# A decoder block on one core: the weights' preparation ahead of the attention loop, rearranged

## The reference

```python
def _act_quant(x):
    s = 127.0 / jnp.clip(jnp.max(jnp.abs(x), axis=-1, keepdims=True), 1e-05)
    return jnp.clip(jnp.round(x * s), -128.0, 127.0) / s
def _weight_quant(w):
    s = 1.0 / jnp.clip(jnp.mean(jnp.abs(w)), 1e-05)
    return jnp.clip(jnp.round(w * s), -1.0, 1.0) / s
qkv = _bitlinear(x, w_qkv).reshape(B, N, 3, H, D)       # both quantized, then x @ w.T
attn = softmax(causal(q @ k.T * D ** -0.5))             # 16 heads of 32
out = _bitlinear(attn @ v, w_proj)
x = x + out; x = x + xattn(layernorm(x), k, bias, ctx); x = x + ffn(layernorm(x))
```

## Time and profile before

| | us |
|---|---|
| three runs | 1494.40, 1491.86, 1492.63 |
| median | 1492.63 |
| profiled execution, span from first to last instruction | 1492.0 |
| PE busy | 1397.0 (94%) |
| DVE busy | 1238.3 (83%) |
| POOL busy | 1181.3 (79%) |
| ACT busy | 867.5 (58%) |
| first `row_max`, t=0 | 61.7 |
| first `low_part`, t=11 | 88.75 |
| end of the last `low_part`, about | 472 |

### The profile page before, as it was taken

One profiled execution on the slowest core, in us unless ns is written; L12 is line 12 of the kernel. 1 busy time (PEld: TensorE's weight loads), 2 busy tenths in 40 slices (PEclk: granted clock), 3 DMA queues, 4 the chain that ended last, 5 costly groups with the idle time before them and its releaser, 6 DMA issues.

```text
span 1492.0 us, 23946 instructions
## 1 busy us (share of the span) xinstructions
PE 1397.0 (94%) x8405; PEld 775.2 (52%) x8405; DVE 1238.3 (83%) x1965; ACT 867.5 (58%) x1433; POOL 1181.3 (79%) x903
## 2 busy tenths in 40 slices
PE   3589999999987898899999999999999999999998
PEld 2478787878764443334444444444444444444443
DVE  5789999999984799889998899899889889898511
ACT  3589999999977223444545455454455446544341
POOL 2379999999986687888888878878887888788432
PEclk9799999999998899999999999999999999999999
DMA  4556464646431633212422321332322232240001
GB/s 144 138 134 157 134 171 133 178 127 165 113 99 48 184 92 84 71 50 71 99 50 50 93 78 43 78 82 60 78 64 71 63 79 57 64 99 14 17 20 29
DMA packets 171587, 133.57 MB, mean 90 GB/s; under 512 B 120500, under 2 KB 124748, under 8 KB 171468
## 3 DMA queue, kind: packets, MB, share of 16 engines
q1 hardware_dynamic: 171276, 131.91, 33.5%
q10 hardware_dynamic: 192, 0.14, 0.1%
HBM read 50.67 MB, written 19.92 MB: 47 GB/s over the span
## 4 chain that ended last, share of the span: by engine, by line
PE 64%; DVE 12%; POOL 8%; ACT 7%; issue 7%; DMA 1%; POOLq 0%; SPq 0%; DVEq 0%; ACTq 0%
PE gu L788 20%; PE gu L802 10%; PE shared_bank L733 9%; PE y L755 3%; PE y L749 3%; PE y L752 3%; PE y L757 3%; PE y L758 3%; POOL pL L1696 3%; DVE blockmax L917 2%; DVE o_sb L957 1%; DVE z L1148 1%; ACT pH L1353 1%; DVE qkt L897 1%; ACT pT L1347 1%
## 5 line engine op out<-in xcount | busy, mean ns | idle before, releaser
L1576 ACT ACTIVATE shared<-shared_bank 128x512 f32<-128x512 f32 x162 | 96.2, 594 | 339.9 <-PE shared_bank L733 339.9
L1145 DVE TENSOR_TENSOR y<-shared,y 128x512 f32<-128x512 f32 x324 | 224.1, 692 | 46.4 <-ACT shared L1576 24.6
L1696 POOL TENSOR_TENSOR pL<-pT,pH 128x768 f16<-128x768 f32 x128 | 216.5, 1693 | 11.1 <-ACT pH L1353 4.9
L788 PE MATMUL gu<-fT,wu 128*128 128x512 f16 x768 | 183.0, 381 | 0.0
L1152 DVE TENSOR_REDUCE oT<-z 128x64 f32<-128x512 f32 x256 | 175.6, 686 | 8.8
L788 PE MATMUL gu<-fT,wg 128*128 128x512 f16 x768 | 181.4, 379 | 1.0 <-DMA fT<-fnl 1.0
L1148 DVE TENSOR_TENSOR z<-y,cT 128x512 f32<-128x512 f32 x236 | 162.4, 688 | 11.6 <-PE y L747 5.3
L1834 POOL TENSOR_TENSOR fuL<-fu,fuH 128x512 f16<-128x512 f32 x96 | 112.3, 1170 | 71.6 <-ACT fuH L1591 71.4
L802 PE MATMUL gu<-wd,fuH 128*128 128x512 f16 x384 | 145.8, 380 | 0.0
L802 PE MATMUL gu<-wd,fuL 128*128 128x512 f16 x384 | 145.6, 379 | 0.0
L1770 POOL TENSOR_TENSOR kv<-vT,cT 128x1024 f32<-128x1024 f32 x70 | 137.9, 1971 | 5.2 <-ACT vT L1531 5.2
(11 more groups left out here) (216 smaller groups left out, 3564.6 us busy)
## 6 DMA issues: line engine op xcount, KB each, us to landing
pack<-qkhl SPq DMA_DIRECT2D x256, 128.0 KB, 2.4
x_sb<-in_x SPq DMA_DIRECT2D x16, 512.0 KB, 4.0
c_sb<-in_ctx SPq DMA_DIRECT2D x32, 256.0 KB, 3.8
hankel<-in_L_xattn_k SPq DMA_DIRECT2D x32, 256.0 KB, 4.1
out_y<-yo SPq DMA_DIRECT2D x32, 256.0 KB, 2.8
x_grp<-x_scratch SPq DMA_DIRECT2D x30, 256.0 KB, 3.4
x_scratch<-x_sb SPq DMA_DIRECT2D x14, 512.0 KB, 2.8
...
```

The lines of the kernel that those rows point to most:

```text
L788: made = T.matmul(bank[:], (wg, wu)[which][:, cb, ib * P:(ib + 1) * P], fT[:, cb, part, :], start=cb == 0 and part == 0, stop=cb == CB - 1 ...
L1145: chain.step(V.tensor_tensor(bank[:], shared[2 * part + half][:], bank[:], op))
L1696: G.tensor_tensor(pL[n % 2][:], pT[n % NP][:], pH[n % NP][:], ALU.subtract).then_inc(low_done, 1)
```

## The change

Sums: chunks 0 and half of 2 are summed by DVE, chunk 1 and the other half of 2 by ACT (`ACT.Abs` with an accumulated output). Chunk 3 is summed by DVE at the end of the prologue. Ternary weights: q's chunk is made by ACT alone (`round_weights(0)`, then a new `sign_weights(0)`), k's by DVE alone (three passes in `ternary(1)`), at the same time; v's by DVE alone (`ternary(2)`), w_proj's by ACT alone, in the loop at t=2. Turning: k first (all four copies by DVE), then q (all four by ACT), in the prologue; v's at t=-3 and -1, w_proj's at t=3 and 4, copied a step later in alternation. The products of batch 0 alternate between q and k. Of the 16 DMAs that pack batch 0, SP issues 8 and ACT 8 (`pack_rest`). v of batch 0 is computed at t=4 and 6, not 0 and 2; piece 0 of the gate weights passes four steps later. POOL fills `pick` and other constants after `power_in(0)`. SP holds back the loads of x(1) and w_proj until chunk 1 is in.

```diff
+        FIRST_V_AT, FIRST_V_SPLIT_AT = (17, 19), (18, 20)
+        V_WEIGHTS_AT, PROJ_WEIGHTS_AT, LOAD_PIECES_AT = (-3, -1), (3, 4), 5
...
+        W_ORDER = (1, 0, 2, 3)
+        def wT_by_act(i, ob):
+            return i == 0 or (i >= 2 and ob % 2 == 0)
+        def turning(t):
+            for i, at in ((2, V_WEIGHTS_AT), (3, PROJ_WEIGHTS_AT)):
+                if t in at:
+                    yield i, range(2 * at.index(t), 2 * at.index(t) + 2)
+        def qk_groups(s):
+            return s % 2, 2 * (s // 2)
...
 tensor_program
-            weight_total([0, 1, 2], 0)
-            turn_weights(0)
-            spread_c(0)
+            bank = misc1.take("tab", w, (tab_done, 1))
+            w.wait_ge(tables_in, 48)
+            T.transpose(bank[:, 0:2 * IB], rows_s[:], ident[0:2 * IB, 0:2 * IB]).then_inc(tab_pe, 1)
+            weight_total(0, 4, 0)
             for j in range(2):
                 turn_xq(0, j)
             turn_weights(1)
+            turn_weights(0)
+            spread_c(0)
             for g2 in range(4):
                 multiply_qk(0, g2)
-            weight_total([3], 1)
-            turn_weights(2)
-            turn_weights(3)
-            spread_c(1)
             for j in range(2):
                 turn_xq(1, j)
+            spread_c(1)
...
+                for i, blocks in turning(t):
+                    turn_weights(i, blocks)
+                if t == V_WEIGHTS_AT[-1]:
+                    weight_total(4, 1, 1)
                 for b, k in project_steps(t):
                     if k < 4:
                         multiply_qk(b, k)
...
 vector_program
             def ternary(i):
-                w.wait_ge(wround_done, i + 1)
+                chain.step(V.tensor_scalar(wraw[i][:], wraw[i][:], ws[:, 1:2], ROUND, ALU.mult, ALU.add))
+                chain.wait()
                 chain.step(V.tensor_scalar(wraw[i][:], wraw[i][:], ROUND - 1.0, ROUND + 1.0, ALU.max, ALU.min))
...
+            magnitude(0, WB, 0)
             max_in(0)
+            magnitude(2, WB // 2, 2)
             scale_in(0)
+            weight_scale(4, 3, 0, 0)
+            ternary(1)
...
+            copy_weights(1)
             stats_in(1)
+            scale_qk(0, 0)
+            scale_qk(0, 1)
+            max_in(1)
+            scale_qk(0, 2)
+            scale_qk(0, 3)
+            scale_in(1)
             ternary(2)
+            magnitude(3, WB, 4)
...
+                for i, blocks in turning(t - 1):
+                    copy_weights(i, blocks)
+                if t == V_WEIGHTS_AT[-1] + 1:
+                    weight_scale(1, 1, 2, 1)
...
 scalar_program
+            def magnitude(i, first, col):
+                w.wait_ge(wraw_in[i], 16)
+                S.activation(tern[i - 1][:, first:WB, :], wraw[i][:, first:WB, :], ACT.Abs, accum_out=wsums[:, col:col + 1]).then_inc(wsum_act, 1)
+            def sign_weights(i):
+                w.wait_ge(act_step, 1 if i == 0 else 2)
...
+                S.activation(tern[i % 2][:], wraw[i][:], ACT.Sign, bias=minus_round[:]).then_inc(tern_act, 1)
+            def pack_rest():
+                w.wait_ge(qk_high, 4)
+                w.wait_ge(qk_low, 4)
+                for r in (2, 3):
+                    for j in range(4):
+                        S.dma_start(packs[0][j * D:(j + 1) * D, :, r, :, :], ...).then_inc(packed[0], 16)
...
             moments(0)
             normalise(0)
+            magnitude(1, 0, 1)
             step_in(0)
+            magnitude(2, WB // 2, 3)
             for i in range(NT):
                 round_in(0, i)
+            round_weights(0)
             diagonal(0)
+            sign_weights(0)
+            for j in range(2):
+                copy_xqT(0, j)
             copy_weights(0)
             copy_c(0)
             moments(1)
             normalise(1)
+            high_qk(0, 0)
+            high_qk(0, 1)
             step_in(1)
+            high_qk(0, 2)
+            high_qk(0, 3)
             for i in range(NT):
                 round_in(1, i)
+            pack_rest()
             diagonal(1)
...
+                if t == PROJ_WEIGHTS_AT[0] - 1:
+                    round_weights(3)
+                    sign_weights(3)
...
 sync_program
-                for r in range(R):
+                for r in range(R) if b > 0 else (0, 1):
...
+            w.wait_ge(wraw_in[1], 16)
             load_x(1)
...
+            pack_qk(0)
...
-                if t == 0:
+                if t == LOAD_PIECES_AT:
                     load_piece(0)
                     load_piece(1)
```

More of the change, by code:

```diff
@@ L497, in tensor_program, with turn_weights @@
             w = Waits(tensor)
-            def turn_weights(i):
-                for ob in range(WB):
-                    freed = (wT_act, 2 * i + ob // 2 + 1) if ob % 2 == 0 else (wT_dve, 2 * i + ob // 2 + 1)
+            def turn_weights(i, blocks=range(WB)):
+                for ob in blocks:
+                    by_act = wT_by_act(i, ob)
                     w.wait_ge(const_done, C_BASE)
-                    bank = misc1.take(("wT", i, ob), w, freed)[:].bitcast(BF16)
-                    w.wait_ge(tern_done, i + 1)
+                    bank = misc1.take(("wT", i, ob), w, (wT_act if by_act else wT_dve, wT_copies(i, ob, by_act)))[:].bitcast(BF16)
+                    if i in (1, 2):
+                        w.wait_ge(tern_dve, i)
+                    else:
+                        w.wait_ge(tern_act, 1 if i == 0 else 2)
                     for cb in range(CB):
@@ L507, in turn_weights, with weight_total @@
                     made.then_inc(wtr_pe, 1)
-            def weight_total(pieces, use):
-                n = len(pieces)
-                bank = misc1.take(("wtot", use), w, (wscale_done, use + 1))
+            def weight_total(first, n, use):
+                bank = misc1.take(("wtot", use), w, (wscale_done, 2 * use + 1))
                 w.wait_ge(const_done, C_BASE)
-                w.wait_ge(wsum_done, pieces[-1] + 1)
-                T.matmul(bank[:, 0:n], ones[:], wsums[:, pieces[0]:pieces[0] + n], start=True, stop=True).then_inc(wtot_pe, 1)
+                w.wait_ge(wsum_dve, 2 + use)
+                w.wait_ge(wsum_act, 2)
+                T.matmul(bank[:, 0:n], ones[:], wsums[:, first:first + n], start=True, stop=True).then_inc(wtot_pe, 1)
             def spread_c(b):
@@ L1229, in scale_down @@
             def scale_down():
-                w.wait_ge(down_in, 16)
+                w.wait_ge(tables_in, 64)
                 chain.wait()
@@ L1319, in round_weights @@
-                S.activation(wraw[i][:], wraw[i][:], ACT.Copy, bias=ROUND, scale=ws[:, 2 * use + 1:2 * use + 2]).then_inc(wround_done, 1)
-            def copy_weights(i):
-                dst, o_first = (wqkvT, i * C) if i < 3 else (wprojT, 0)
-                for ob in range(0, WB, 2):
-                    w.wait_ge(wtr_pe, WB * i + ob + 1)
-                    src = misc1.of["wT", i, ob][:].bitcast(BF16)[:, 0:CB * P].rearrange("p (c o) -> p c o", c=CB)
-                    S.activation(dst[:, :, o_first + ob * P:o_first + (ob + 1) * P], src, ACT.Copy).then_inc(wT_act, 1)
+                w.wait_ge(wscale_done, 2 * use + 1)
@@ new lines, in copy_weights @@
+            def copy_weights(i, blocks=range(WB)):
+                dst, o_first = (wqkvT, i * C) if i < 3 else (wprojT, 0)
+                for ob in blocks:
+                    if wT_by_act(i, ob):
+                        w.wait_ge(wtr_pe, w_turned(i, ob))
+                        src = misc1.of["wT", i, ob][:].bitcast(BF16)[:, 0:CB * P].rearrange("p (c o) -> p c o", c=CB)
+                        S.activation(dst[:, :, o_first + ob * P:o_first + (ob + 1) * P], src, ACT.Copy).then_inc(wT_act, 1)
@@ L1713, in gpsimd_program @@
             power_in(0)
+            set_pick()
+            set_once()
+            power_in(1)
             for g2 in range(4):
                 low_qk(0, g2)
[L1716 to L1723 removed]
             for t in STEPS:
```

182 lines of the change are left out of this document (87 added, 95 removed).

## The result

The changed kernel takes 1504.24 us (median of 4 runs, 1504.13 to 1504.32), the kernel before, beside it, 1493.26 (4 runs, 1491.86 to 1494.4). The ratio is 1.0073, interval [1.0059, 1.0087]: 0.73% slower. The forecast was 1496.0 with a range up to 1500.5, so the sign of the likeliest case was right and the size wrong by 8 us.

The account below looks back on a forecast made before the run. It took POOL as the pace from t=11, DVE just before, batch 2's input ahead of that. -8.1 + 3.9 + 1.8 + 4.1 + 1.8 = +3.5 us on 1492.0, plus 0.6 to the median, gave 1496.0, range 1486.5 to 1500.5.

Parts of the forecast that it names:

- the six terms of the table: Forecast shifts from `max_in(2)` through `take_max(0)`, `take_max(4)`, `low_part(0)`, `low_part(8)` to the last `low_part`: -8.1, +3.9, +1.8, +4.1, +1.8, 0 us.
- Scale, q's and k's weights, packing start: Prologue: scale ready at 16.7 us, `multiply_qk(0)` at 26.7, packing from 37.35, instead of 18.34, 32.41 and 40.98.
- I take the middle, 48.2: Batch 2's statistics start at 48.2 us, between 46.5 (load alone) and 50.0; so `max_in(2)` at 53.0, -8.1.
- the bound 50.0 for shared DMA engines: Batch 2's statistics start at 50.0 us if 16 packing DMAs hold the DMA engines 9.3 us, whoever issues; sum 1.8 worse.
- Steps up to `take_max(0)`, 8.7: `max_in(2)` to `take_max(0)`: 8.7 us instead of 4.75, +3.9 (+1.0 to +4.5), as turned weights take banks among products.
- `take_max(0)` to `take_max(4)`, 12.6: 12.6 us instead of 10.75, +1.8 (+0.4 to +2.5): PE waits for ACT's two w_proj passes before turning its blocks.
- `take_max(4)` to `low_part(0)`, +4.1: +4.1 us (0 to +4.7): DVE's v splits and piece 0's mask and clamp now come at t=5 to 7.
- POOL, "0 to +3.6, I take +1.8": After `low_part(0)`: piece 0's add and take, 1.82 us each, move to steps 15 and 16, where POOL is full; +1.8.
- Later, 0: From `low_part(8)` to the last `low_part`: no further change, 0 us.
- (3): Rival, much slower: ports hold POOL's last low part (+2.4), shared DMA engines delay batch 2 (+1.8); 1500.3 us, chance 0.10.
- (2): Rival, faster: ACT's pair and bank waits hidden, steps lose only DVE's added work; -6.1 to -4.4, 1487.4 us, chance 0.28.

Follow-up runs that it names:

- e14_before_x_early: The kernel before with only x(2) loaded ahead of the first batch's packing; 1493.55 us.
- e2_x2_early: The changed kernel with x(2) loaded right behind w_proj, ahead of the packing; 1495.15 us.
- e5_v_turned_ahead: The changed kernel with v's weights turned behind `spread_c(1)` at the prologue's end and all four blocks copied there by VectorE; 1500.26 us.
- e12_proj_late: e11_piece_late with w_proj turned at steps 3 and 4 instead of -3 and -1; 1499.84 us.
- e16_w_proj_turned_first: e7 plus x(2) loaded before the packing, all packing DMAs on SP, w_proj's sum on ScalarE, w_proj turned at steps -6 and -5; 1482.84 us.
- e3_proj_ahead: The changed kernel with w_proj's total, scale, rounding and sign at the end of the prologue; 1502.28 us.
- e10_v_late: e7 with the first batch's V products and splits at the change's late steps; 1493.36 us.
- e13_piece_late_loaded_early: e11_piece_late with the first two pieces loaded at step 0 again, piece 0's passes still late; 1495.37 us.
- e1: The changed kernel with all 16 packing DMAs of batch 0 issued by SP, none by ACT; 1507.0 us.
- e11_piece_late: e7 with the first pieces loaded at step 5 and piece 0 four steps later, as in the change; 1501.73 us.
- e7: The changed kernel with v's turns and w_proj's ternary in the prologue, w_proj turned at -3 and -1, early piece loads, V and piece 0 at old steps; 1492.04 us.
- e4: The changed kernel with the first batch's V products at their projection's steps 14 and 16, splits at 15 and 17; 1505.98 us.
- e6: e3_proj_ahead with w_proj turned at steps 0 and 1, first pieces loaded at step 2, piece 0 in its old steps; 1506.52 us.

## Why the prediction was wrong

The chain was the right one: each term of the sum has the forecast sign, and what it said would be seen (PE waiting for ACT at t=3, VectorE idle beside it, `low_part(0)` after 89) is there. It failed in size. Of the six terms of the table five came out worse for the change, by 1.3 to 1.7 us each, and one better by 0.3: 6.9 us in all. In two of them (batch 2's load, POOL) the working named a cause and its price, and I took the middle between that price and nothing. At their full price the sum would have given 1499.7, so the middles are 3.6 us of the miss. In two more (`take_max(4)` to `low_part(0)`, and the attention after `low_part(16)`) most of the cost goes with a stretch of half clock that the sum didn't have.

- **Scale, q's and k's weights, packing start.** 16.45, 25.85 and 36.23 against 16.7, 26.7 and 37.35: right, a little better. The turns at the port are there, and more than one: `ternary(2)`'s passes took 1.41, 2.07 and 2.06 us against 1.23, and POOL's four low parts 6.46 us where one alone takes 1.16. The Trainium skill (SBUF — State Buffer, Who interferes with whom) says that whoever comes first holds the shared pair for the whole instruction, and the trace agrees.
- **"I take the middle, 48.2."** This step failed. Measured 49.88, beside the bound 50.0 for shared DMA engines. The Trainium skill (DMA: Bandwidth & Descriptors, Issuing engines are not separate DMA queues) spoke for that bound: two issuers save only issue time. The trace agrees: the issue ends 5.4 us earlier, the load is used 2.0 us earlier, and the share is 1.06. The earlier trace rows had warned with 0.89. How the prediction came from 9.3 us of packing behind 37.35 to 48.1, and not 46.7, it doesn't say, so that the bound fits to 0.1 us is partly luck. The load also wasn't the gate in the kernel before: VectorE's last instruction ahead of the statistics starts at 56.19 there, and `e14_before_x_early` gains nothing. The change frees VectorE at 39.4, and it then stands idle for 10.46 us until the load; `e2_x2_early` shows what that is worth: 9 us.
- **Steps up to `take_max(0)`, 8.7.** Measured 9.91. The mechanism (a bank between the products) is shown by `e5_v_turned_ahead` (5.62), `e12_proj_late` (4.95) and `e16_w_proj_turned_first` (4.98) against 7.50 to 10.17 wherever a weight is turned there. 0.76 of the missing 1.2 us is one product of a single column at 61.79, 0.93 us where the same one takes 0.17 in `e5_v_turned_ahead`: it ends at 62.72, with POOL's low part of 61.55 to 62.71.
- **`take_max(0)` to `take_max(4)`, 12.6.** Measured 12.21, and `e3_proj_ahead` takes away 2.6 of it with ACT's pair. That the number fits is partly luck: the pair ended 0.9 us sooner than forecast (+7.4 instead of +8.3), and the product behind the turn took 1.91 us at half clock where the sum has 1.05.
- **`take_max(4)` to `low_part(0)`, +4.1.** Measured +5.5. Up to `take_max(8)` it is +4.32: the four split operations 2.9, mask 0.7, clamp 0.9 and a copy 0.3, less some 0.5 of idle that was there before; that part is as forecast. The other +1.2, behind `take_max(8)`, was not in the sum. It goes with PE at half clock (0.50 from 87.0 to 90.4): the nine profiled runs with half clock in that stretch take 4.98 to 6.02 us for it, the ten others 3.80 or 3.81, `e10_v_late` with the same late V among them.
- **POOL, "0 to +3.6, I take +1.8".** Measured +3.1, and +3.0 in `e13_piece_late_loaded_early`. The reason for less than the whole (POOL's gaps in steps 11 and 12 are made good later) is what failed: a gap that stays empty is lost for the engine that sets the pace.
- **Later, 0.** Measured +1.5. From `low_part(16)` to `low_part(108)` both kernels take 283.5 us; from there to `low_part(112)` the changed one takes 12.70 and the kernel before 11.03. There, from 431.8 to 435.2, the granted clock is 0.50, and w_proj's four products take 1.87 us:

```profile
431.20:435.20 4.00, 3.99 (x22) 2.46 (x23) 2.48 (x3) 1.49 (x3) 2.18 (x2) 0.57 0.00 2
...
433.47 1.87 PE L669 MATMUL misc<-wprojT,oqT 128*128 128x512 bf16 x4
```

In the kernel before, at the same place:

```profile
422.30:426.30 4.00, 3.94 (x48) 3.10 (x49) 3.80 (x9) 2.06 (x5) 2.83 (x3) 1.00 0.00 0
...
423.80 1.03 PE L630 MATMUL misc<-wprojT,oqT 128*128 128x512 bf16 x4
```

The five profiled runs with such a stretch between 421 and 439 us (the changed kernel, e1, e2, e3, e10) take 335.3 to 335.5 us from `low_part(16)` to the last; twelve without it take 333.4 to 334.2. `e11_piece_late` and `e12_proj_late` (335.5) lose it in the last two steps, where the clock is halved for 6.8 us from 468 on. PE was as busy in the 4 us ahead of it in the changed kernel (2.01) as in the kernel before (2.05), so why the clock falls in one and not in the other stays open.

The parts of the loss, by `low_part(8)` and by the time:

| step | `low_part(8)` | median |
|---|---|---|
| all moved steps undone (e7 against the changed kernel) | -11.3 | -12.2 |
| v's turns ahead (e5 against the changed kernel) | -2.3 | -4.0 |
| w_proj's ternary ahead (e3 against the changed kernel) | -1.4 | -2.0 |
| V late (e10 against e7) | +0.65 | +1.3 |
| piece 0's passes late (e13 against e7) | +3.5 | +3.3 |
| piece 0's load late too (e11 against e13) | +5.7 | +6.4 |

They start from two kernels and don't have to add up. In the changed kernel the late load alone costs no wait: VectorE comes to the mask at 81.69, when the load is there. In e3, e4, e6, e11 and e12, where it comes earlier against the load, it waits 1.1 to 10.7 us. So in the changed kernel an earlier delay hides the late load, and taking that delay away, as e3 does, shows less than its own price.

Of the rivals, (3), much slower, 1500.3, was nearest: it added the shared DMA engines (+1.8, true) and a longer hold of POOL's low parts, which did not come. (2) said that VectorE is given only 1.9 us more and has the room for it; it counted by the mean over a stretch whose first half has room and whose second has none.
